# Additive attention written out: pairs of steps share one tanh, and three of four projections move into the first iteration

## The reference, cut to what matters

```
# h: [8, 512, 128]; x = layernorm(h)
k = x @ Wx;  q = x @ Wt                                   # 64 units
t = tanh(q[:, :, None, :] + k[:, None, :, :] + bt)        # 512 x 512 x 64 per sequence
e = exp(t @ Wa + ba)                                      # [b, i, j]
h = h + (e / (sum_j e + 1e-7)) @ x
# then, on layernorm(h): 8 experts of 256, the best 2 by a router
g = x @ w_gate[e];  u = x @ w_up[e];  y = (silu(g) * u) @ w_down[e]
h = h + sum over the best two of weight * y
```

## Time and profile before

| what | us |
|---|---|
| median of 3 runs | 2662.2 |
| profiled execution | 2676.98 |
| its span | 2675.9 |
| ACT busy over the span | 1408.7 |
| DVE busy over the span | 1892.2 |
| PE busy over the span | 2031.4 |
| stretch of the 16 iterations | 916.5 to 2076.0 |

### The profile page before, as it was taken

One profiled execution on the slowest core, in us unless ns is written; L12 is line 12 of the kernel. 1 busy time (PEld: TensorE's weight loads), 2 busy tenths in 40 slices (PEclk: granted clock), 3 DMA queues, 4 the chain that ended last, 5 costly groups with the idle time before them and its releaser, 6 DMA issues. The chain is left out here.

```text
span 2675.9 us, 38480 instructions
## 1 busy us (share of the span) xinstructions
PE 2031.4 (76%) x11944; PEld 1013.6 (38%) x11944; DVE 1892.2 (71%) x5013; ACT 1408.7 (53%) x1685; POOL 290.4 (11%) x339
## 2 busy tenths in 40 slices
PE   5988869688737567899999888988999877543750
PEld 2566544466613112333333333333333533232640
DVE  1655544566569878999999899889999577576332
ACT  0222222123104499999999899999999321000320
POOL 5000011100100100000000000000000000054246
PEclk9899979878558788999999999999999988766875
DMA  6000020000100200000000000000000000311532
GB/s 231 15 0 0 0 112 0 18 1 1 48 0 24 81 1 1 1 1 1 1 1 1 2 1 1 1 2 1 1 1 1 4 3 1 139 47 36 168 107 74
DMA packets 52327, 75.67 MB, mean 28 GB/s; under 512 B 8112, under 2 KB 36160, under 8 KB 51392
## 3 DMA queue, kind: packets, MB, share of 16 engines
q1 hardware_dynamic: 43136, 46.35, 5.0%
q0 software_dynamic: 8736, 23.10, 2.7%
q10 hardware_dynamic: 288, 4.19, 0.4%
HBM read 40.07 MB, written 23.07 MB: 24 GB/s over the span
## 5 line engine op out<-in xcount | busy, mean ns | idle before, releaser
L1470 ACT ACTIVATE KM<-KM 128x2048 f32<-128x2048 f32 x464 | 876.3, 1930 | 58.0 <-DVE KM L1328 57.6
L1328 DVE TENSOR_SCALAR KM<-big 128x512 f32 (+1 forms) x1856 | 759.1, 483 | 28.8 <-PE bank L1564 8.6
L1564 PE MATMUL bank<-KM,w_a_wa 128*32 128x512 f32 x4096 | 562.5, 627 | 145.6 <-ACT KM L1470 123.4
L238 POOL TENSOR_TENSOR nrstd<-nrstd,minus_half 128x4 f32<-128x4 f32 (+1 forms) x90 | 88.8, 999 | 2001.5 <-DVE nrstd L215 1952.4
L1564 PEld LDWEIGHTS bank<-KM,w_a_wa 128*32 128x32 f32 x4096 | 83.5, 110 | 508.8 <-ACT KM L1470 384.0
L1555 PE MATMUL bank<-rf_wgu,XT 128*128 128x512 f32 x512 | 274.8, 621 | 0.0
L1387 DVE SCALAR_TENSOR_TENSOR t512b<-ST,rf_w,bank 128x256 f32<-128x256 f32 x256 | 123.1, 481 | 15.9
L1383 DVE SCALAR_TENSOR_TENSOR ST<-ST,bank 128x256 f32<-128x256 f32 x256 | 107.0, 418 | 30.3 <-ACT ST L1459 28.4
L1466 ACT ACTIVATE KM<-big 128x512 f32 (+1 forms) x192 | 124.3, 757 | 0.0
L1459 ACT ACTIVATE ST<-bank 128x256 f32<-128x256 f32 x256 | 103.3, 404 | 28.2 <-PE bank L1555 28.2
L222 DVE TENSOR_SCALAR XN<-h,nmv,nrstd 128x128 f32 (+1 forms) x296 | 80.5, 348 | 38.4 <-POOL nrstd L238 23.1
(11 more groups left out here) (347 smaller groups left out, 3172.5 us busy)
## 6 DMA issues: line engine op xcount, KB each, us to landing
queues<-zeros SPq DMA_DIRECT2D x1, 8192.0 KB, 22.5
KM<-queues SPq DMA_DIRECT2D x32, 256.0 KB, 2.8
results<-KM POOLq DMA_DIRECT2D x32, 256.0 KB, 2.6
big<-XN SPq DMA_DIRECT2D x24, 256.0 KB, 2.6
KM<-in_task_W ACTq DMA_DIRECT2D x2, 2048.0 KB, 10.7
w<-in_w SPq DMA_DIRECT2D x1, 4096.0 KB
big<-in_w_pairs SPq DMA_DIRECT2D x1, 4096.0 KB
big<-XT SPq DMA_DIRECT2D x8, 256.0 KB, 2.3
```

The source lines that it names most:

```text
L238: self.nc.gpsimd.tensor_tensor(self.m.nrstd[s][:, 0:self.tiles], self.m.nrstd[s][:, 0:self.tiles], self.m.minus_half[:, 0:self.tiles], ALU ...
L1328: last = nc.vector.tensor_scalar(ARG[step % NBUF][:, cc, :], KU[:, bass.ds(i * T, T)], q, None, ALU.add)
L1470: nc.scalar.activation(ARG[step % NBUF], ARG[step % NBUF], ACT.Tanh).then_inc(th.sem, 1)
L1564: last = nc.tensor.matmul(m.bank[g][32 * cc:32 * cc + 32, :], w["a_wa"][:, 30 - 2 * k:62 - 2 * k], ARG[step % NBUF][:, cc, :], start=k == ...
```

## The change

- The four step buffers become three buffers of two steps each (two KM tiles and a new tile aa_args), so that DVE may write step s once PE has used step s - 6.
- ACT works on pairs of steps: at each even step it takes one tanh over 4096 columns, for this step and the next, after both sets of arguments are there. For steps 12 and 13 it is one of 2048 and four biased ones, for 22 and 23 eight biased ones. PE waits once for each pair of steps.
- Only pair 0 is projected ahead of the iterations. Pairs 1, 2 and 3 are projected inside iteration 0, beginning at steps 2, 12 and 22, through other PSUM banks.
- All loops of the stage are written out on every engine.

The lags of gates, products, turns and copies, and the tables above, stay.

```diff
-    NBUF = 4
+    NBUF = 3
+    FULL = CS // 2
-    ARG = [m.KM[n // 2][:, 4 * (n % 2):4 * (n % 2) + 4, :] for n in range(NBUF)]
+    more = ctx.sb("aa_args", [P, 8, T])
+    ARGS = [m.KM[0], m.KM[1], more]
+    ARG = lambda n, step: ARGS[(n * FULL + step // 2) % NBUF][:, 4 * (step % 2):4 * (step % 2) + 4, :]
+    PROJ = (2, 12, 22)
...
             def arguments(n, i, step):
-                if step >= NBUF or has(n, 1):
-                    dve.wait_ge(used.sem, used.at(n, step - NBUF + 1))
+                if n * FULL + step // 2 >= NBUF:
+                    dve.wait_ge(used.sem, used.at(n, step - 2 * NBUF + 1))
...
                 for step in range(CS):
+                    if n == 0:
+                        for k in range(len(PROJ)):
+                            project(k + 1, step - PROJ[k])
...
+            def tanh(n, i, full):
+                own = [step for step in (2 * full, 2 * full + 1) if step not in BIASED]
+                if own:
+                    act.wait_ge(arg.sem, arg.at(n, args_before(own[-1]) + 1))
+                if len(own) == 2:
+                    a = ARGS[(n * FULL + full) % NBUF][:, :, :]
+                    last = nc.scalar.activation(a, a, ACT.Tanh)
+                if len(own) == 1:
+                    last = nc.scalar.activation(ARG(n, own[0]), ARG(n, own[0]), ACT.Tanh)
...
+                last.then_inc(th.sem, 1)
...
-                    elif attention:
-                        act.wait_ge(arg.sem, arg.at(n, args_before(step) + 1))
-                        nc.scalar.activation(ARG[step % NBUF], ARG[step % NBUF], ACT.Tanh).then_inc(th.sem, 1)
+                    if attention and step % 2 == 0:
+                        tanh(n, i, step // 2)
+                    if n == 0:
+                        for k in range(len(PROJ)):
+                            project(k + 1, step - PROJ[k])
...
-                        pe.wait_ge(th.sem, th.at(n, step + 1))
+                        if step % 2 == 0:
+                            pe.wait_ge(th.sem, th.at(n, step // 2 + 1))
...
-            with pe.Fori(1, PAIRS) as i:
-                for c in range(NC_):
-                    iteration(i * NC_ + c, i * (2 * NC_) - (0 if c else 2 * NC_), c)
```

More of the change, by code:

```diff
@@ L1272, in has @@
     def has(n, back):
-        return not isinstance(n, int) or n >= back
+        return n >= back
     def begun(t, lag):
@@ L1312, in _ @@
             nc.gpsimd.memset(zero[:, :], 0.0).then_inc(zeroed.sem, 1)
[L1313 to L1316, removed]
+            for i in range(PAIRS):
+                norm.gpsimd(pool, i)
+            for n in range(COUNT):
                 norm2.gpsimd(pool, n)
@@ L1459, in units @@
                     nc.scalar.activation(TH(u), GU(u)[:, 0:H], ACT.Tanh, scale=0.5).then_inc(th_sb.sem, 1)
+            def tanh(n, i, full):
[7 more added lines that the diff above has]
+                    last = nc.scalar.activation(ARG(n, own[0]), ARG(n, own[0]), ACT.Tanh)
+                for step in (2 * full, 2 * full + 1):
+                    if step in BIASED:
+                        if n * FULL + full >= NBUF:
+                            act.wait_ge(used.sem, used.at(n, step - 2 * NBUF + 1))
+                        for cc in range(CG):
+                            last = nc.scalar.activation(ARG(n, step)[:, cc, :], KU[:, i * T:(i + 1) * T], ACT.Tanh, bias=query(n, step, cc))
+                last.then_inc(th.sem, 1)
@@ new lines, in project @@
+            def project(i, step):
+                if step == 6:
+                    for s in S:
+                        act.wait_ge(xt_ps.sem, xt_ps.at(i, s + 1))
+                        if i:
+                            act.wait_ge(kq_ps.sem, kq_ps.at(i - 1, 2))
+                        nc.scalar.copy(XT[s][:, :], m.bank[3 + s][:, :]).then_inc(xt_sb.sem, 1)
+                if step == 8:
+                    act.wait_ge(kq_ps.sem, kq_ps.at(i, 1))
+                    nc.scalar.copy(KU[:, i * T:(i + 1) * T], m.bank[5][:, :]).then_inc(kq_sb.sem, 1)
+                    act.wait_ge(kq_ps.sem, kq_ps.at(i, 2))
+                    nc.scalar.activation(QU[:, i * T:(i + 1) * T], m.bank[6][:, :], ACT.Identity, bias=w["a_bt"][:, 0:1]).then_inc(kq_sb.sem, 1)
@@ L1481, in _ @@
                 act.wait_ge(m.loaded[name], 16)
[L1482 to L1494, removed]
+            for step in range(9):
+                project(0, step)
+            for n in range(COUNT):
+                iteration(n, n // NC_, n % NC_)
             iteration(COUNT, None, 0, attention=False)
@@ L1511, in attend @@
                 pe.wait_ge(et.sem, et.at(n, 2))
+                pe.wait_ge(xa_kept.sem, 32 * (n // NC_ + 1))
                 for s in S:
@@ L1597, in _ @@
                     pe.wait_ge(zeroed.sem, 1)
-                iteration(n, 0, n)
-            with pe.Fori(1, PAIRS) as i:
-                for c in range(NC_):
-                    iteration(i * NC_ + c, i * (2 * NC_) - (0 if c else 2 * NC_), c)
+                    pe.wait_ge(kq_sb.sem, 2 * PAIRS)
+                iteration(n, (n - 1) // NC_ * (2 * NC_), n % NC_)
             iteration(COUNT, (PAIRS - 1) * 2 * NC_, 0, attention=False)
```

66 lines of the change are left out of this document (41 added, 25 removed).

## The result

| | before | after |
|---|---|---|
| median, us | 2662.1 (4 runs, 2661.5 to 2663.7) | 3119.4 (4 runs, 3117.2 to 3124.5) |
| profiled execution, its span | 2676.98, 2675.9 | 3124.54, 3122.9 |

The ratio is 1.172, 95% interval 1.170 to 1.174. The time was forecast at 3180, with a range of 3060 to 3240. L1474 is now the tanh of 4096 columns, L1331 the arguments, L1466 the gate, L1386 and L1390 the gate's products, L1609 the scores of a step, L1446 the exp of scores.

What follows compares the result with a forecast made beforehand. ACT, DVE and PE were taken as close to full, with DVE setting the pace. Fourteen iterations growing from 73.8 to 110.6 us give 515, the rest +2; +517 us on the median makes 3180 us, range 3060 to 3240.

Steps and rivals of the forecast that it cites:

- The chain: From one merged tanh to the next: tanh, gate, product, arguments in series, 6.49 us; an iteration takes 105.6 us.
- pair f: Steps 2f and 2f+1 of an iteration; each of the sixteen pairs was given an interval between tanh starts.
- the clock: PE, idle some 3 us in each pair, drops to its slow clock; 5 us per iteration added, making 110.6.
- F: Length of one tanh over 4096 columns on ACT, taken as 3.51 us, between 3.40 and 3.61.
- the ten intervals that the even steps bind: Intervals beginning after pairs 1, 3, 4, 5, 7, 8, 9, 11, 12, 13; 74.1 us together.
- the three chains that I had run through a slow PE: Turned scores (+0.9 to 1.4 us), attend (+0.9 to 2.9) and expert sum (+1.7 to 3.3).
- one gap: In the trace before, 2.05 us of PE idle time, then scores of a step at 1.94 instead of 1.07 us.
- the likeliest's own range: Range of the forecast case itself, chance 0.65: 3130 to 3240 us.
- the clock's lower end: The clock stays up and adds 0 us per iteration instead of 5: 70 us down.
- the rival with the full clock: PE keeps its full clock, an iteration takes 105.6 us and the kernel 3105 us; chance 0.22.
- The rest: Outside the steady iterations: projections -19 us at the first tanh, iteration 0 +11, iteration 1 +10; +2 us.
- No buffer takes part: No buffer is in the chain from tanh to tanh, so the third one cannot shorten its 6.49 us.

## Why the prediction was right, and where its sum was off

**The chain: right.** Thirteen of the sixteen intervals came out within a tenth of a microsecond. The starts of ACT's tanh in iteration 4 give the intervals below; that of pair 15 ends at the next iteration's first tanh.

| pair f | predicted | measured | | f | predicted | measured |
|---|---|---|---|---|---|---|
| 0 | 3.5 | 3.52 | | 8 | 6.96 | 6.97 |
| 1 | 7.06 | 7.10 | | 9 | 7.06 | 7.05 |
| 2 | 7.7 | 7.68 | | 10 | 3.8 | 3.79 |
| 3 | 6.96 | 6.96 | | 11 | 8.4 | 8.33 |
| 4 | 10.0 | 9.60 | | 12 | 6.49 | 6.48 |
| 5 | 6.49 | 6.48 | | 13 | 7.8 | 7.58 |
| 6 | 5.0 | 5.01 | | 14 | 4.0 | 3.99 |
| 7 | 7.0 | 6.97 | | 15 | 7.5 | 8.49 |

The sum is 106.0 against 105.6 without the clock. The misses are pairs 4 and 13, 0.4 and 0.2 too long in the forecast, and pair 15, whose terms add to 7.4 and not to the 7.5 that I wrote. F is 3.51: 7.13 us for two tanh in a row less 3.62 for one. Pairing alone gives the loss, DVE's order takes nearly all of it back, and the third buffer changes it by 0.4%. Beginning the units at odd steps shortens nine of the ten intervals that the even steps bind, by 17 us together in its iteration 4, while pair 4, with the wait for the attended sum, grows from 9.6 to 12.4.

**The clock: the term that was mis-sized.** I added 5 us per iteration, 70 in all. The experiment that kept TensorE busy ahead of pair 15 measured 1.4 net per iteration, 20 in all; its shortest iterations, 104.5 us, are 2.1 below the mean of the changed kernel, and more than this no run here gives for the clock. Of the three chains that I had run through a slow PE, two ran at full clock in every full iteration but n = 2: in iteration 5, for one, the scores ahead of turning (step 4) and of attending took 1.06 and 1.07 us, after 1.56 and 0.51 us of idle time. Pair 4 was longer all the same in iterations 7 and 12 (10.6 us), where PE came late to these scores from work at a granted clock of 0.50. I had taken the term from one gap, as if every gap of such a length slowed PE. The sum with the net 1.4 for 5, less 0.5 for pair 15 (6.98 at full clock) and 0.4 for pair 4, is 106.0, and 14 x 4.6 = 64 us off 3180 make 3116; 3119.4 was measured.

The forecast was thus right in its mechanism and lay 61 us too high. 3119.4 is below the 3130 with which the likeliest's own range began, though the clock's lower end alone, 70 us off 3180, would have reached 3110. It lies in the stated range because this took in the rival with the full clock, and that rival's 3105 was nearer than the forecast. The Trainium skill ("TensorE: Matmul & The Clock Gate", section on HAM oscillation) says that bursts of matmuls parted by waits can each begin at the slow clock. Pair 15 agrees, with a granted clock of 0.50 after 5.07 us of idle time; the scores ahead of turning and attending did not do so.

**The rest: right in its numbers, in part by luck.** The first tanh comes 18.6 us earlier against what ran before the stage (predicted 19). Iteration 0 is +11.9 and iteration 1 +9.7 (predicted +11 and +10). That +11.9 is what the projections cost is not shown: with pairing alone and no projections in it, iteration 0 has +13.3 (with two pair buffers), and with one tanh per step and the projections in it, +15.4. The two loop stalls of 3.5 us went; no run shows apart what that was worth.

**"No buffer takes part": right for the steady iterations of this kernel.** With two pair buffers they have the same mean as with three. Where fewer tanh are merged a buffer can matter: it was 1.5 of the 4.0 us that three merged tanh cost. What the prediction had only as a term of the gate's chain holds by itself as well: a merged tanh waits for the arguments of its second step, too, and all that DVE does between the two stands ahead of it, even when no gate is late. That was 2.35 us for steps 28 and 29, with four buffers or six, and 1.66 for steps 16 and 17.

A merged tanh saved 0.10 us (3.51 against 2 x 1.805). What it cost has no fixed size: 2.3 us each in the changed kernel (32.6 for fourteen), 1.3 and 0.9 for three with four and six buffers, 0.3 with DVE's arguments first. The remark of the Trainium skill that breaking up instructions may let work complete sooner ("Perfetto Trace Analysis", Optimizing Scalar/DVE Operations) agrees with these: the same kernel with one tanh per step has a ratio of 0.991 instead of 1.172.

## What to carry to other kernels

Before instructions are merged on an engine, write down for each engine in program order what stands behind the first thing that waits for the merged result; if the next input of the same engine is there, the merged length, and not the average load, sets the interval. Write down as well what stands between the inputs of the instructions to be merged, since the merged one waits for the last of them. Here, with three engines above 90% busy, a saving of 0.10 us per instruction was never worth this. Put an instruction that waits for another engine behind the work that the busiest engine will need next: three such moves on DVE took the ratio from 0.991 to 0.982 here, with no instruction saved.

## What the hardware showed that I had not expected

The length of PE's idle time alone does not say whether its clock falls. In iteration 4 of the changed kernel eight scores took 1.07 us after 3.18 us of idle time, and sixteen took 3.40 and 3.43 after 2.65 and 5.07. In iteration 8 the scores of the same step (20) took 1.93 after the same 3.18:

```profile
1292.33 3.40 PE L1609 MATMUL bank<-KM,w_a_wa 128*32 128x512 f32 x16 [2.65 <-ACT KM L1474]
...
1324.81 1.07 PE L1609 MATMUL bank<-aa_args,w_a_wa 128*32 128x512 f32 x8 [3.18 <-ACT aa_args L1474]
...
1750.62 1.93 PE L1609 MATMUL bank<-KM,w_a_wa 128*32 128x512 f32 x8 [3.18 <-ACT KM L1474]
```

PE alone in single microseconds of the last two and of pair 15 (length, busy, granted clock, of which 1.00 is the 2.4 GHz level and 0.50 the 1.2 GHz level):

```profile
1324.80:1325.80 1.00, 0.99 (x8) 1.00 0.00 0
...
1751.00:1752.00 1.00, 1.00 (x8) 0.50 0.00 0
...
1351.00:1352.00 1.00, 1.00 (x8) 0.50 0.00 0
```

What decides between them stays open; no run here varied it.
